# Local attention: where the first score block and the first half of a turned item stand in TensorE's order

## What is computed

```python
q = heads(x @ Wq.T); k = heads(x @ Wk.T); v = heads(x @ Wv.T)      # 32 heads of 8
kw = jnp.concatenate([kp[:, :, :-1], kp[:, :, 1:]], axis=3)        # block before, own block
vw = jnp.concatenate([vp[:, :, :-1], vp[:, :, 1:]], axis=3)
scores = jnp.einsum('bhnrd,bhncd->bhnrc', qb, kw) * scale
valid = (dist >= 0) & (dist <= window) & (key_global >= 0)
scores = jnp.where(valid, scores, lowest)
out = jnp.einsum('bhnrc,bhncd->bhnrd', softmax(scores), vw)
```

## Time and profile before

| | us |
|---|---|
| median of 3 runs | 421.43 (419.5 to 421.68) |
| the profiled execution | 422.58 |
| its span | 420.7 |
| local attention, from the projections (119.6) to the last turned item (222) | about 102 |
| TensorE busy | 366.4 (87%) |
| VectorE busy | 301.1 (72%) |
| ScalarE busy | 206.2 (49%) |

### The profile page before, as it was taken

The page is one execution under the profiler, slowest core; times in us unless marked ns, Lnnn a source line. Parts: engine busy times, 40 slices in busy tenths (PEclk is TensorE's granted clock), DMA queues, the critical chain, the costliest instruction groups (busy, mean ns, idle before and its releaser), DMA issues.

```text
span 420.7 us, 6955 instructions
## 1 busy us (share of the span) xinstructions
PE 366.4 (87%) x2438; PEld 227.6 (54%) x2438; DVE 301.1 (72%) x624; ACT 206.2 (49%) x549; POOL 111.3 (26%) x214
## 2 busy tenths in 40 slices
PE   8897958699996999989977757778989889999995
PEld 3645546544452566556754423436657645666774
DVE  4999788977634687897878987898888466522355
ACT  2765411450036765774444747989989643101100
POOL 7437778657571000000020111121111000000003
PEclk9879995979999799999978878999999999999998
DMA  7994111832660000020022698999899710412231
GB/s 202 384 371 110 2 3 2 240 60 38 163 299 0 2 2 2 2 51 2 2 47 56 123 151 163 166 164 148 166 147 156 218 34 5 134 50 76 50 100 50
DMA packets 90306, 43.52 MB, mean 103 GB/s; under 512 B 78945, under 2 KB 86049, under 8 KB 89825
## 3 DMA queue, kind: packets, MB, share of 16 engines
q1 hardware_dynamic: 87968, 43.02, 43.2%
q0 software_dynamic: 2304, 0.07, 1.5%
HBM read 21.58 MB, written 2.88 MB: 58 GB/s over the span
## 4 chain that ended last, share of the span: by engine, by line
PE 53%; DVE 11%; DMA 11%; ACT 10%; issue 8%; POOL 6%; SPq 1%; POOLq 0%; DVEq 0%; ACTq 0%
PE ps L840 26%; ACT area_a L750 6%; PE ps L1079 6%; PE ps L1321 6%; DMA area_b<-area_a 5%; PE ps L1093 5%; POOL deltas L544 3%; PE ps L1073 3%; PE ps L1011 3%; DMA area_b<-deltas 2%; DMA early<-in_w_qkv_dram 2%; DVE area_a L1724 2%; DMA deltas<-entry_w,small 2%; ACT area_a L725 1%; PE ps L849 1%
## 5 line engine op out<-in xcount | busy, mean ns | idle before, releaser
L1724 DVE CUSTOM_DVE_ANT_0 area_a<-ps,zero,small 128x1024 f32<-128x1024 f32 x64 | 79.5, 1276 | 10.0 <-PE ps L1143 7.4
L750 ACT ACTIVATE area_a<-area_a,small 128x1024 int16<-128x1024 f32 x64 | 73.1, 1143 | 22.6 <-POOL small L598 13.2
L840 PE MATMUL ps<-xT_odd,early 128*128 128x128 f32 (+2 forms) x248 | 61.8, 394 | 4.4 <-ACT area_a L761 1.8
L725 ACT ACTIVATE area_a<-ps,small 128x256 f32<-128x256 f32 (+1 forms) x128 | 51.9, 430 | 28.3 <-DVE small L1673 26.0
L522 POOL TENSOR_SCALAR var_eps<-meanvar 128x1 f32<-128x1 f32 x24 | 8.1, 336 | 181.9 <-DVE meanvar L1452 181.8
L840 PEld LDWEIGHTS ps<-xT_odd,early 128*128 128x128 f32 x248 | 38.6, 190 | 25.9 <-ACT area_a L761 5.9
L1673 DVE TENSOR_REDUCE small<-ps 128x4 f32<-128x1024 f32 (+1 forms) x24 | 29.3, 1221 | 19.1 <-PE ps L1079 18.9
L598 POOL TENSOR_SCALAR small<-small 128x1 f32<-128x1 f32 x64 | 12.6, 197 | 87.8 <-DVE small L1724 87.7
L840 PE MATMUL ps<-area_b,xT_even 128*128 128x512 f32 x64 | 30.5, 641 | 3.9 <-ACT area_b L702 3.9
L1807 DVE TENSOR_TENSOR area_b<-ps,area_b 128x384 f32<-128x384 f32 (+1 forms) x16 | 9.2, 573 | 33.7 <-ACT area_b L808 33.7
L1682 DVE COPY area_b<-ps 128x512 f32<-128x512 f32 x48 | 30.9, 681 | 2.8 <-PE ps L1093 2.6
(11 more groups left out here) (285 smaller groups left out, 634.9 us busy)
## 6 DMA issues: line engine op xcount, KB each, us to landing
early<-in_w_up_dram SPq DMA_DIRECT2D x1, 4096.0 KB, 12.3
area_b<-gates_out SPq DMA_DIRECT2D x16, 256.0 KB, 3.1
deltas<-area_b SPq DMA_DIRECT2D x1, 2112.0 KB, 14.6
area_b<-deltas SPq DMA_DIRECT2D x2, 1024.0 KB, 6.4
area_a<-in_w_down_dram SPq DMA_DIRECT2D x1, 2048.0 KB, 9.7
area_b<-area_a SPq DMA_TRANSPOSE x67, 3.3
early<-in_ctxT_dram SPq DMA_DIRECT2D x1, 1024.0 KB, 11.2
early<-in_ctx_dram SPq DMA_DIRECT2D x1, 1024.0 KB, 15.0
```

Of the source, the lines that this page charges most:

```text
L725: a = act.activation(p1[:, n % 2, x * nk * P:(x + 1) * nk * P], scores1(n)[:, x * nk * P:(x + 1) * nk * P], ACT.Exp, bias=nmx1[:, n % 2, x ...
L750: act.activation(px[:, u % PX, :], sx[:, u % 3, :], ACT.Exp, bias=nbx[:, u:u + 1], accum_out=zx[:, i, h:h + 1]).then_inc(sem("px_ready"), 1)
L840: mm = pe.matmul(dst, lhsT(c), rhs(c), start=start and c == 0, stop=stop and c == DC - 1, **kw)
L1724: dve.tensor_tensor_reduce(sx[:, u % 3, :], bank(2 * (u % 2), 2), zero[:].broadcast_to([P, B * M]), qsc[:, i, h:h + 1], LOWEST, ALU.add, A ...
```

## The change

Three things are rewritten in `stage4`, and no arithmetic:

- TensorE computes `scores(0)` right behind the four projection blocks, with a wait for the c = 0 half of queries and keys alone. `local_values(3)` and the turning of the rounded values follow it, then `scores(1)`. The wait for the placed values moves from ahead of `scores(0)` to the first `apply1`.
- VectorE takes `maxima(0)` ahead of `place_values(1)`, and both `place_rounded_values` ahead of `maxima(1)`.
- For the single-tile items `turn(n)` is cut in two: its first half stands ahead of `scores(n + 2)`, its second half behind it. Each half of item 0 waits for its own bank alone.

```diff
--- before.py
+++ after.py
@@ -1000,6 +1000,8 @@
                 i, c, hh, _ = items1[2 * m]
                 nk = 1 + i % 2
                 pe.wait_ge(sem("pT1_ready"), 4 * (m + 1))
+                if m == 0:
+                    pe.wait_ge(sem("v1_ready"), TT // 2)
                 if i and 2 * m == first1[i]:
 
                     pe.wait_ge(sem("sums1_out"), i)
@@ -1056,12 +1058,12 @@
                 for c in range(DC):
                     for k, w in ((0, wq1), (1, wk1)):
                         dense(bank(2 * c + k), lambda d: w[:, d, c * P:(c + 1) * P], lambda d: xT[1][:, d, :]).then_inc(sem("qk1_ps"), 1)
-                local_values(TT - 1)
-
-                for c in range(DC):
+
+                def turn_rounded_values(c):
                     for k in range(KT):
                         mm = pe.transpose(bank(4 + c).bitcast(BF16)[:, k * P:(k + 1) * P], ivT[:, c, k * P:(k + 1) * P], ident_b[:])
                     mm.then_inc(sem("iv_ps"), 1)
+
                 def scores(n):
                     i, c, hh, gp = items1[n]
                     nk = 1 + i % 2
@@ -1080,29 +1082,35 @@
                                            start=False, stop=b == nk - 1)
                     mm.then_inc(sem("s1_ps"), 1)
 
-                def turn(n):
-                    if n == 0:
-
-                        pe.wait_ge(sem("ivtok_ready"), DC)
-                    for x in range(2):
+                def turn(n, halves):
+                    for x in halves:
                         pe.wait_ge(sem("p1_ready"), 2 * n + x + 1)
                         if n:
 
                             pe.wait_ge(sem("pT1_ready"), 2 * n + x - 1)
+                        else:
+
+                            pe.wait_ge(sem("ivtok_ready"), x + 1)
                         for y in range(4):
                             mm = pe.transpose(bank(4 + x)[:, y * P:(y + 1) * P], p1[:, n % 2, (4 * x + y) * P:(4 * x + y + 1) * P], ident[:])
                         mm.then_inc(sem("pT1_ps"), 1)
 
 
+                pe.wait_ge(sem("qT1_ready"), 1)
+                pe.wait_ge(sem("kT1_ready"), 1)
+                scores(0)
+                local_values(TT - 1)
+                for c in range(DC):
+                    turn_rounded_values(c)
                 pe.wait_ge(sem("qT1_ready"), DC)
                 pe.wait_ge(sem("kT1_ready"), DC)
-                pe.wait_ge(sem("v1_ready"), TT // 2)
-                scores(0)
                 scores(1)
                 for n in range(len(items1)):
+                    first_half = 1 if items1[n][0] % 2 == 0 else 0
+                    turn(n, range(first_half))
                     if n + 2 < len(items1):
                         scores(n + 2)
-                    turn(n)
+                    turn(n, range(first_half, 2))
                     for i in range(TT - 1):
                         if n == first1[i + 1] + 1:
                             turn_z1(i)
@@ -1662,7 +1670,6 @@
                 scale_queries(0)
                 place_values(0)
                 scale_queries(1)
-                place_values(1)
 
                 def maxima(n):
                     nk = 1 + items1[n][0] % 2
@@ -1682,9 +1689,10 @@
                         dve.tensor_copy(pT1[:, n % 4, 4 * x * P:4 * (x + 1) * P], bank(4 + x)).then_inc(sem("pT1_ready"), 1)
 
                 maxima(0)
+                place_values(1)
                 place_rounded_values(0)
+                place_rounded_values(1)
                 maxima(1)
-                place_rounded_values(1)
                 for n in range(len(items1)):
                     for i in range(TT - 1):
                         if n == first1[i + 1] + 1:
```

## The result

The changed kernel takes 428.53 us, median of four (424.02 to 435.86), against 421.56 before: ratio **1.013**, interval 1.0067 to 1.0194. The forecast was 421.1 within 419.0 to 424.2. So it is slower by 0.5 to 1.4%, with one interval that just reaches no change. Ratios and intervals leave out executions in a slower state, in either kernel; medians take in all, so a ratio can differ from that of the medians by up to 0.6%.

What follows compares the result with a forecast made beforehand. It took TensorE's standstills and slow clock at the start and at items 12 to 15 as the limit; -2.28 + 1.91 = -0.37 us from the median of 421.43 gave 421.1, range 419.0 to 424.2.

Steps and rivals of the forecast that it cites:

- Part 1: Start of local attention: scores(0) right behind the projections, so scores(2) may start at 132.35 instead of 135.07, 2.72 us earlier.
- The loop of 4.18 us: Single-tile items: scores, maxima, copy, half, next scores form one trip through TensorE and VectorE, 4.18 us for each item.
- Loss at items 12 to 15, 1.91: Items 12 to 15: halves wait for VectorE's copies, so scores(18) comes at 194.06 instead of 192.15, 1.91 us lost.
- Gain at the start, 2.28: Start of local attention: scores(6) comes at 146.98 instead of 149.26, 2.28 us won.
- I take full clock there: Start of local attention: TensorE's pauses of about 1.3 to 1.5 us, not 2.67 in one piece, leave the clock full.
- The price of the low clock: In the trips: 5.95 us each at 1.2 GHz; a 7 us spell holds 1.2 trips and costs 2.1 us.
- The first rival: Clock falls in the new pauses: one spell 423.2, two (start, items 12 to 15) 425.3; chances 0.12 and 0.08.
- The second rival: Start: before's low clock is an accident of some executions; part 1 wins 0.5, sum +1.4, 422.8 or above; chance 0.10.
- The third: The half doesn't hold up the scores: start gains 4.5, rear loses nothing, 416.9 us; chance 0.10.

Runs made afterwards that it cites:

- before kept busy: Kernel before, plus nine idle TensorE products nobody reads in its 2.67 us pause ahead of scores(2): 420.31 us, ratio 0.9980.
- halves only: Kernel before, plus only the first half of each single-tile item turned ahead of the next scores: 429.65 us, ratio 1.0183.
- first scores only: The change without halves in front: scores(0) early and VectorE's new order, every item turned whole; 417.17 us, ratio 0.9864 to before.
- halves at tile 2 only: The change with halves in front for items 12 to 15 alone: 419.96 us, ratio 0.9974 to before.
- the second profile of the change: The change unaltered, run again for another profile and five more rounds: 424.66 us, ratio 1.0046 to before.
- trips kept busy at start: The change plus four idle TensorE products ahead of the first halves of items 1 and 2 each: 425.48 us, ratio 1.0071 to before.
- the copy ahead: The change, plus VectorE's copy of a single-tile item's first half ahead of the next maxima: 416.34 us, ratio 0.9850 to before.

## Why the prediction was wrong, step by step

- **Part 1, scores(0) ahead, 2.72 us:** right, 8.63 - 5.91 = 2.72, within 0.01 in every profile with it. The order of VectorE's small steps and the moved wait cost nothing, as said.
- **The loop of 4.18 us:** right in mechanism and size, 4.13 to 4.14 at full clock, and gone when the copy was moved.
- **Loss at items 12 to 15, 1.91:** right, 1.94, at full clock.
- **Gain at the start, 2.28:** right for the execution that was profiled first, 2.41. But it counts against an execution of before that had a spell. Against before without one (before kept busy, 20.73) it is 0.32.
- **"I take full clock there":** this step failed. The prediction reasoned that several pauses are safer than one of 2.67. (It put them at 1.3 to 1.5 us. Its own working, 4.18 less 1.58 and 1.02, gives 1.58; 1.43 was measured.) The trips at the start stand unfilled in five profiles, and in four of them the clock was low there, in three from a fall within the trips and in one (halves only) from a fall just ahead of them. At items 12 to 15 it fell in one of the six profiles that have the trips there unfilled. Falls at the start aren't peculiar to trips: before, first scores only and halves at tile 2 only, with their items turned whole, show one too.
- **The price of the low clock, +2.1 for a spell of 7 us:** the price of a trip without `apply1` was right (5.95 against 5.94 and 5.96). A trip with it took 6.7 to 6.8, which the prediction left out, so that a spell of 7 us cost the second profile of the change 2.7 (23.11 - 20.41). The length was wrong too. It was taken from before, where the items are turned whole and the spell ends after 7 us. With the trips it lasted 10, 17 and 20 us in three profiles, and 7 in two. In items turned whole it lasted 3 to 7. The first rival named the right cause. With the 7 us that low clock in the trips of one place cost in two profiles (halves only at the start, trips kept busy at items 12 to 15), it would have given 428 instead of 423.2; in the change's own three profiles the clock cost 0, 2.7 and 3.3 us. I gave the rival 0.20 in all. The passage in the Trainium skill that I had set against the change ("TensorE: Matmul & The Clock Gate", the section "A second HAM failure mode: psum-queue depth-cycling") tells of a clock that swings between its levels. The traces agree that it falls where pauses are short and frequent. They differ in that it fell once at a place and then stayed low for 7 to 20 us, and in that no profile has it low at both places.
- **The second rival**, that the spell of before is an accident, was right in its size (2.1 us, it took 1.8), and I had set it too low. Without that spell it forecast the change 1.4 us slower; with the clock kept up in both kernels the local attention is 1.76 slower. How many executions of before have the spell isn't known: taking it away won 2.1 us in the profile and 1 in the median.
- **The third**, the half that holds nothing up, named what the copy ahead then did on purpose: scores(6) at 17.91, where it had 18.4 (144.8 - 126.44).

So two things stand behind the miss: the clock, which idle products in the waits bring back, 4.7 us on the chip where both were measured side by side, and, by the profiles of the local attention alone, a gain at the start that was counted against a slow spell of before. How often the clock falls at each place in executions that aren't profiled stays open: their mean clock takes in the falls in other stages, too. That the idle products at items 12 to 15 brought the median from 425.48 to 422.45 (on different chips, with overlapping ranges of single times) suggests that it falls there in more than the one execution whose profile caught it. Why the same kernel gave 1.013, 1.0046 and 1.0136 is not shown.

## What to carry to other kernels

A piece of work that is pulled ahead in one engine's list brings its waits with it: ask what stands behind it, and move the partner's step on the other engine as well, or it becomes a loop through both. Here, on one chip, that made the difference between 0.5% slower and 1.5% faster. Ask too what the piece pulled ahead wins by itself: the halves in front added nothing clear to the 1.4% of the first scores alone, even with the partner moved. A gain that is read against a slow spell of the kernel before counts only for the executions that have that spell. Where a change leaves TensorE waiting a little in each of several items, price them at 1.2 GHz for as long as the items last, and take the profile of one execution as one draw.

## What the runs showed of the hardware that I had not expected

- The granted clock fell to 1.2 GHz with no pause longer than 0.82 us ahead of it, in two profiles (first scores only, and halves at tile 2 only). In both it was 1.00 up to 133 and 0.62 over 133 to 137.5, with TensorE busy for 4.2 of the 5 us before.
- At 1.2 GHz in the trips TensorE was busy for 17.24 of 19.5 us (halves only) and for 15.75 of 16.5 (trips kept busy at start), and the clock stayed low. It was back at full within 1 us of the scores behind the last trip in the four profiles with low clock in the trips at the start, and 5.6 us behind them in the one at items 12 to 15.
- Eighteen idle products of 512 columns (1.03 us for four, 1.47 for six), placed in waits, kept the clock at 1.00 through both places in the one profile taken, at no delay of the real work: scores(6) at 20.41 and 24.77 us for items 12 to 18, as without them at full clock (20.41 and 24.76).
- The same local attention, in three executions of the change, had no low clock, 7 us of it and 10 us of it, and took 83.20, 85.89 and 86.49 us.
